# Two bands in one PSUM bank, and the projection's stores issued by SyncE

## The reference, cut to what matters

```python
# x: (16, 192, 56, 56); n = 49 tokens per window, 64 windows per image
qkv = fq(xw) @ fq(Wqkv, axis=0).T + bqkv          # xw: (1024, 49, 192), qkv: 576 columns
q, k, v = jnp.split(qkv, 3, axis=2)
q = fq(q * SCALE); k = fq(k); v = fq(v)           # three maxima over all of q, k, v
attn = fq(fq(attn) + bias); out = softmax(attn) @ v
out = fq(out) @ fq(Wout, axis=0).T + bout         # the projection, back to (16, 192, 56, 56)
# second part: depthwise 7x7 convolution, layer norm, two products with GELU and GRN,
# and the residual that was kept:  return residual + y
```

## Time and profile before

| | us |
|---|---|
| median of 3 runs | 5082.19 |
| lowest, highest | 5073.92, 5095.0 |
| the profiled execution, its own time | 5095.38 |
| its span, first to last instruction | 5093.7 |
| range stage | about 165 to 450 |
| projection stage | about 2479 to 3005 |

### The profile page before, as it was taken

The page is one execution under the profiler, slowest core; times in us unless marked ns, Lnnn a source line. Parts: engine busy times, 40 slices in busy tenths (PEclk is TensorE's granted clock), DMA queues, the critical chain, the costliest instruction groups (busy, mean ns, idle before and its releaser), DMA issues. The chain is left out here.

```text
span 5093.7 us, 116728 instructions
## 1 busy us (share of the span) xinstructions
PE 4027.8 (79%) x40394; PEld 2551.1 (50%) x40394; DVE 3922.3 (77%) x7112; ACT 3246.1 (64%) x5602; POOL 1504.5 (30%) x1844
## 2 busy tenths in 40 slices
PE   1687777676688988888456669996689999999999
PEld 1233554454577776777444434443345455554544
DVE  7797999999999999999645520001799999999985
ACT  0675777775698988989355644443556666666663
POOL 0201111111666666666422200001232222222210
PEclk9997777876799999999777779998799999999999
DMA  7773666665333333333277778886122222222212
GB/s 316 203 204 107 160 160 166 159 163 143 79 96 94 91 94 91 94 91 94 74 256 254 279 243 290 278 278 200 63 66 90 87 90 76 76 90 87 90 55 68
DMA packets 227952, 725.18 MB, mean 142 GB/s; under 512 B 30346, under 2 KB 128138, under 8 KB 206794
## 3 DMA queue, kind: packets, MB, share of 16 engines
q1 hardware_dynamic: 203402, 589.58, 39.6%
q0 software_dynamic: 24128, 130.26, 7.1%
HBM read 428.25 MB, written 291.50 MB: 141 GB/s over the span
## 5 line engine op out<-in xcount | busy, mean ns | idle before, releaser
L852 POOL TENSOR_TENSOR exp_lo<-exp,exp_hi 128x294 f16<-128x294 f32 x1024 | 773.1, 782 | 374.8 <-ACT exp_hi L923 374.8
L1613 PE MATMUL out_psum<-gelu_hi,w_parts 128*128 128x448 f16 x2016 | 605.0, 355 | 58.9 <-DVE w_parts L1789 31.5
L1649 ACT ACTIVATE gelu_pair<-h_psum,b_rows,w_unscale 128x448 f32<-128x448 f32 x448 | 324.5, 728 | 412.5 <-PE h_psum L1565 224.7
L1685 DVE BATCH_NORM_STATS2 ln_stats<-z_img 128x6 f32<-128x192 f32 x448 | 126.0, 344 | 566.7 <-DMA z_img<-zd 565.9
L1349 PE MATMUL conv_psum<-c_in,toeplitz 128*128 128x448 f16 (+1 forms) x2304 | 470.4, 366 | 68.9 <-DMA dwb<-in_L_conv_dw_b_dram 68.9
L948 DVE SCALAR_TENSOR_TENSOR logit_int<-attn_int,scalars,bias_products 128x588 f16<-128x588 int8 x512 | 488.2, 954 | 38.6 <-ACT attn_int L929 27.0
L1565 PE MATMUL h_psum<-ln_parts_T,w_hi 128*128 128x448 f16 x2016 | 494.3, 354 | 18.1 <-DVE w_in L1748 16.2
L929 ACT ACTIVATE attn_int<-p_psum,scalars 128x588 int8<-128x588 f32 x512 | 389.4, 761 | 174.7 <-PE p_psum L455 163.7
L1613 PE MATMUL out_psum<-gelu_lo,w_parts 128*128 128x448 f16 x1344 | 475.5, 354 | 0.0
L610 PE MATMUL range_psum<-q_diag,k_diag 128*128 128x196 bf16 x1536 | 275.2, 316 | 227.8 <-DVE p_min L692 225.0
L894 PE MATMUL o_psum<-a_v,exp_hi 128*128 128x34 f16 x6144 | 382.8, 179 | 78.4 <-DVE a_o L975 66.3
(11 more groups left out here) (313 smaller groups left out, 9901.8 us busy)
## 6 DMA issues: line engine op xcount, KB each, us to landing
k_diag<-kd SPq DMA_DIRECT2D x128, 384.0 KB, 5.0
toeplitz<-gd SPq DMA_DIRECT2D x48, 1024.0 KB, 17.2
yd<-y_out POOLq DMA_DIRECT2D x16, 2880.0 KB, 28.1
c_in<-yd SPq DMA_DIRECT2D x24, 1920.0 KB, 9.4
zd<-c_out POOLq DMA_DIRECT2D x24, 1792.0 KB, 13.8
z_img<-zd SPq DMA_DIRECT2D x16, 2688.0 KB, 9.4
x_chunk<-in_x_dram SPq DMA_DIRECT2D x12, 3136.0 KB, 10.4
x_img<-in_x_dram SPq DMA_DIRECT2D x16, 2352.0 KB, 15.9
```

The costliest lines, as they stand in the source:

```text
L852: last = nc.gpsimd.tensor_tensor(el[r][:, :, 2 * a, 0:N], src[:, :, a], eh[r][:, :, 2 * a, 0:N], ALU.subtract)
L1613: last = nc.tensor.matmul(po[:, t, 0:TCH], w, hx[:, f, cols], start=f == 0 and x == 0, stop=f == NF - 1 and x == len(steps) - 1)
L1649: nc.scalar.activation(h[y // 2 % 3][:, y % 2], ph[:, y % 3, 0:TCH], ACT.Gelu, scale=k1[:], bias=b1[:, f:f + 1]).then_inc(hd, 1)
```

## The change

**Range stage.** Two bands share the bank of the half-empty chunk: PAIR = 9 steps per two bands instead of 10. The ninth step writes the 64 live columns of chunk 4 for band b into partitions 0 to 63 and those of band b + 1 into partitions 64 to 127, with four matmuls of 64 weight columns. STEPS falls from 40 to 36, NG from 10 to 9. Since 9 is odd, the bank halves alternate from image to image. Five groups per image keep 8 matmuls, four have 10. The last reduction becomes two, a copy fills the scales' upper half, and the all-reduce waits for 14 links instead of 12.

**Projection stage.** (1) GpSimd quantizes units 0 and 1 before its memsets and the all-reduce, and units 2 and 3 after the all-reduce, before it issues the weights' transfers. (2) VectorE places bands 0 to 3 of image 0 before it waits for the all-reduce, and bands 4 to 7 after the chain. (3) The stores of `y_out` and `r_out` are issued by SyncE, between its loads, in a fixed order, and six units are loaded ahead of the loop. (4) The residual is stored in two parts (chunks 0 to 3, and 4 to 6), with a semaphore each; ScalarE waits for the first at x = 0 and for the second at x = 8.

```diff
@@ phase_qkv_range
-    STEPS = NWIN * NCH
+    PAIR = 2 * (NCH - 1) + 1
+    STEPS = NWIN // 2 * PAIR
...
-            pool.wait_ge(ch1, 12)
+            pool.wait_ge(ch1, 14)
...
-                        b, j, gg = n // NCH, n % NCH, n // GRP
+                        x, gg, slot = n % PAIR, n // GRP, (STEPS * k + n) % 8
...
-                        for t in range(2):
-                            rows = CK + NPART if t == 0 else CK
-                            last = nc.tensor.matmul(ps[:, n % 8, 0:BAND], s.wT[t][:, j * P:(j + 1) * P],
-                                                    xi[k][0:rows, t, b * BAND:(b + 1) * BAND], start=t == 0, stop=t == 1)
+                        b, j = n // PAIR * 2 + x % 2, x // 2
+                        whole = j < NCH - 1
+                        for lo, hi, bb in ((0, P, b),) if whole else ((0, 64, b), (64, P, b + 1)):
+                            for t in range(2):
+                                rows = CK + NPART if t == 0 else CK
+                                last = nc.tensor.matmul(ps[lo:hi, slot, 0:BAND], s.wT[t][:, j * P:j * P + hi - lo],
+                                                        xi[k][0:rows, t, bb * BAND:(bb + 1) * BAND], start=t == 0, stop=t == 1,
+                                                        skip_group_check=not whole)
...
-                        v.tensor_reduce(stat[:, gg * GRP:(gg + 1) * GRP], ps[:, gg % 2 * GRP:(gg % 2 + 1) * GRP, 0:BAND], AX.X, ALU.max,
+                        half = (NG * k + gg) % 2
+                        v.tensor_reduce(stat[:, gg * GRP:(gg + 1) * GRP], ps[:, half * GRP:(half + 1) * GRP, 0:BAND], AX.X, ALU.max,
...
@@ phase_project, SyncE
+            def store_r(m, k, part, lo, hi):
+                dst = s.rd[bass.ds(m, 1)].rearrange("i (t p) n -> (i p) t n", t=2)
+                sp.dma_start(dst[:, :, lo:hi], r[k][:, :, lo:hi]).then_inc(strr[k][part], 16)
+
+            def image(i, loads):
+                for k in range(2):
+                    m = 2 * i + k
+                    if loads(k):
+                        load(2 * m + 6, 0, False)
+                    sp.wait_ge(re, 2 * NTC * m + 2 * RTOP)
+                    store_r(m, k, 0, 0, RTOP * TCH)
+                    if loads(k):
+                        load(2 * m + 7, 1, False)
+                    sp.wait_ge(ye, NY * (m + 1))
+                    sp.dma_start(s.yd[:, :, bass.ds(m, 1)].rearrange("b p i c x q -> p (b i) (c x q)"),
+                                 y[k][:].rearrange("p (b c) x q -> p b (c x q)", c=CB)).then_inc(sty[k], 16)
+                    sp.wait_ge(re, 2 * NTC * (m + 1))
+                    store_r(m, k, 1, RTOP * TCH, TOK)
+
+            for u in range(6):
+                load(u, u % 2, u < 2)
...
@@ phase_project, ScalarE
-                        if not first and x == 0:
-                            act.wait_ge(strr[k], 16 * i)
+                        if not first and x in (0, 2 * RTOP):
+                            act.wait_ge(strr[k][x // (2 * RTOP)], 16 * i)
...
@@ phase_project, VectorE
+            dve.wait_ge(ones, 5)
+            for b in range(NWIN // 2):
+                place(0, 0, b, True)
             dve.wait_ge(ar, 1)
...
-            for b in range(NWIN):
+            for b in range(NWIN // 2, NWIN):
                 place(0, 0, b, True)
```

More of the change, by code:

```diff
@@ L405, in _ @@
             link(v.memset(sel[:, 2, 3:4], 1.0))
-            link(v.memset(sel[0:64, 2, 4:5], 1.0))
+            link(v.memset(sel[:, 2, 4:5], 1.0))
             def image(i, first):
@@ L1040, in phase_project @@
         sty = [s.sem(f"y_stored{k}") for k in range(2)]
-        strr = [s.sem(f"r_stored{k}") for k in range(2)]
+        strr = [[s.sem(f"r_stored{k}_{p}") for p in ("top", "rest")] for k in range(2)]
         oqd, tr, otd = s.sem("o_quantized"), s.sem("o_transposed"), s.sem("oT_placed")
@@ L1068, in _, with load @@
             sp.wait_ge(ones, 3)
-            def image(i, first):
-                for k in range(2):
[L1072 to L1078, removed]
+            def load(u, hf, first):
+                if not first:
+                    sp.wait_ge(oqd, u - 1)
+                for h in range(2):
+                    sp.dma_start(oi[hf][64 * h:64 * h + N], s.od[bass.ds(u, 1)].rearrange("u h n j w f -> (u h) n j w f")[h]).then_inc(ld[hf], 16)
+            def store_r(m, k, part, lo, hi):
+                dst = s.rd[bass.ds(m, 1)].rearrange("i (t p) n -> (i p) t n", t=2)
+                sp.dma_start(dst[:, :, lo:hi], r[k][:, :, lo:hi]).then_inc(strr[k][part], 16)
+            def image(i, loads):
+                for k in range(2):
+                    m = 2 * i + k
[12 more added lines that the diff above has]
+                load(u, u % 2, u < 2)
+            with sp.Fori(0, IMG // 2 - 2) as i:
+                image(i, lambda k: True)
+            image(IMG // 2 - 2, lambda k: k == 0)
+            image(IMG // 2 - 1, lambda k: False)
+            for k in range(2):
+                sp.wait_ge(sty[k], 16 * IMG // 2)
+                for part in range(2):
+                    sp.wait_ge(strr[k][part], 16 * IMG // 2)
         @blk.gpsimd
@@ L1085, in _ @@
                 link(nc.gpsimd.memset(oi[k][:], 0.0))
[L1086 to L1091, removed]
-            for x in range(2):
-                for t in range(2):
-                    nc.gpsimd.dma_start(s.gd[x, t * CK:(t + 1) * CK, :], lines[x][:, t, :]).then_inc(lst, 16)
             def quantize(u, hf, first):
@@ L1211, in _, with place @@
                 v.memset(y[k][:, :, :, QP], 0.0).then_inc(otz, 1)
+            def place(m, k, b, early):
+                dve.wait_ge(tr, NWIN * m + b + 1)
+                if not early and b == 0:
+                    dve.wait_ge(ym, NY * (m - 1))
+                    dve.wait_ge(rm, 2 * NTC * (m - 1))
+                for t in range(2):
+                    src = pt[0:CK, b % 2, :, 64 * t:64 * t + N].rearrange("p w (y x) -> p w y x", x=WS)
+                    dst = backwards(ot[k][t], 7 * b + 1, [[WS, NWIN], [PITCH, WS], [1, WS]], CK)
+                    v.tensor_scalar(dst, src, OFF, None, ALU.subtract).then_inc(otd, 1)
             dve.wait_ge(otz, 6)
```

41 lines of the change are left out of this document (20 added, 21 removed).

## The result

| | before | after |
|---|---|---|
| median, us | 5084.95 (5 runs, 5073.92 to 5095.0) | 5054.46 (5 runs, 5049.21 to 5066.06) |
| profiled span, us | 5093.7 | 5064.4 |

After / before is 0.994, 95% interval 0.9926 to 0.9953: 30.5 us faster, with 24 to 38 in the interval. The forecast was 5059, from 5082.19.

What follows compares the result with a forecast made beforehand. Reduction and round trip together bound the range stage, seven gapless DMA engines the projection stage. Terms -7.7 + 0.4 - 10 - 5 + 4.3 - 5 = -23.0 took the median 5082.19 to 5059 us, range 5037 to 5081.

Steps and rivals of the forecast that it cites:

- the term of three slots: Range stage: four narrow matmuls take three slots instead of the two of two wide ones, +0.17 us per ten-matmul group.
- The switches: Range stage: changing between full and half width loses some 0.09 us each way, +0.18 us per ten-matmul group.
- the two edge groups: Range stage: in two of four ten-matmul groups one switch falls into the wait, so each costs +0.26 us, not 0.35.
- Rival B: Range and projection stages: switches cost nothing and one queue feeds seven engines evenly, 0.5 to 1 us less per image; 5037, chance 0.20.
- The gap of 5.5: Projection start: ScalarE's 5.50 us idle for the third quantization goes, as units 2 and 3 follow the all-reduce; -5 us.
- it comes at 2510.6: Projection start: the all-reduce comes at 2510.6, 3.6 us later than now, behind two quantizations and 5.5 us of memsets.
- sign of being wrong: Projection stage: the forecast is wrong if the time per image moves by over 1 us either way.
- seven engines set the cadence: Projection loop: seven DMA engines have no gap and set the time per image, 30.4 us by the rows, 29.2 measured.
- The rise of 4.3 us in rows: Projection stores: y_out's 3072 rows take 8.70 us in the hardware queue, +0.27 per image, +4.3 us in all.
- 8.7 + 3/7 x 6.9: Projection end: y_out's rows plus the residual's remaining three sevenths, within 17.3 us from last store to next stage; -5 us.
- C (stores bring nothing): Projection stores bring nothing, or range-stage narrow matmuls do not pair: 5070 or 5081, taken at 5072 us; chance 0.18.
- D (SyncE held): Projection loop: y_out's store holds SyncE 13.7 us, loads come late, 3.75 us more per image, 5119 us; chance 0.14.

Runs made afterwards that it cites:

- e12: Changed kernel with band b + 1's two narrow matmuls left out of each shared bank, band b's kept narrow; nine reductions take 16.07 us against 16.11.
- e5: Changed kernel with two wide matmuls instead of four narrow ones per shared bank, band b + 1's last 64 columns left out; range stage 287.2 us against 298.5.
- e3: Kernel before with units 0 to 3 quantized early and bands 0 to 3 placed early, stores left with GpSimd, residual whole; ratio to before 0.9984.
- e4: Kernel before with y_out and residual stores issued by SyncE, residual in two parts, nothing early; ratio to before 0.9986.
- e2: Kernel before with the new projection stage alone; ratio to before 0.9967.
- e6: Changed kernel with each load of 49 partitions cut into 48 and 1; median 4983.2 us, ratio to before 0.9786.
- e8: Changed kernel with the residual's second part issued ahead of the y_out store; last store to stage end 12.6 us instead of 20.8.
- e10: Changed kernel with loads of 48 and 1 partitions and all stores issued by GpSimd after the image's last piece; ratio to before 0.9898.
- e7: Changed kernel with GpSimd's oT memsets ahead of the two early quantizations; first y_out piece 51.8 us after the stage's start, 4 later than in after.

## Why the prediction was right or wrong

**Sign, size and range: right.** 5054.5 lies 4.5 us under the forecast and within its own range. That it is so near is partly luck. The changed stages gained 39.4 us in the profiled pair (16 + 24 in the mean of the kernels) against 23 forecast, while the runs of the whole kernel say 24 to 38; what becomes of the rest is not shown. And the terms are off both ways: range stage, rows and missing terms brought 23 us more than forecast, start and end 7 less.

**Range stage, -7.7 forecast (-7.3 with its end), -17.0 measured: the term of three slots.** It took only the second matmul of the lower half and the first of the upper to pair. The trace of after shows both pairs, so two slots, and in e12 leaving out the upper half of them saves next to nothing. That is 0.17 us in four groups of sixteen images, 10.9 us. The switches were sized nearly right, 0.18 forecast against 0.22, and so were the two edge groups: e5 has all at 11 us, forecast 2 x 0.18 + 2 x 0.09 = 0.54 us per image, 8.6 us. Rival B came near this stage's size for another reason (free switches, three slots): switches are not free, 0.09 us each.

**Start, -15 forecast, -11.9 measured.** The gap of 5.5 went as forecast (first piece to first store, 30.0 to 24.1). The first piece came 6.0 earlier, not 10: the step "it comes at 2510.6", 31 us after the stage's start, failed. The all-reduce came after 38.3, with 7.25 us ahead of it that the profile explains by nothing. Before, such time would have lain under the wait of 10.22 us for VectorE's chain; the memsets now end after that chain and leave it open. Of the 7.2 us 4 showed, as the forecast had VectorE placing bands 0 to 3 until 34.6, behind the all-reduce; it placed them ahead of it.

**Missing term, -6.3.** From first to third store the stage gained this much more. The forecast said that the DMA engines start earlier and priced only the compute engines. e3 and e4 show that either part alone does it (57.8 to 52.1 and 50.7). Another 2.9 us came between the 13th store and the last (70.3 to 67.3); their cause is open.

**Cadence, +0.27 us forecast, -0.01 measured**, which is less than the scatter between executions. By the forecast's own sign of being wrong, 1 us either way, e2 with 31.36 would have refuted it and after not, though the code is the same. The claim that matters, that seven engines set the cadence, e6 bears out. The rise of 4.3 us in rows is not seen. The software queue's packets were 4800 bytes, not 960 (547 packets for 2.63 MB in the earlier trace rows, 220 ns each in the mean); the hardware queue's are 960 bytes of 45 ns. Per 960 bytes that is 44 against 45, and alone both ran at 350 GB/s.

**End, -5 forecast, -1.3 measured.** The step "8.7 + 3/7 x 6.9" put the residual's second part right behind `y_out`. In fact it held SyncE for 10.8 us, and the end came 10 us behind that. In e2, with the same code, it held 6.3 us and the end was 16.4, near the 17.3 forecast; e8, without it, has 12.6.

**Rivals.** B's cadence, 0.5 to 1 us less, is within what e5 and e12 read (28.6) and not after, so it is not decided. C (stores bring nothing): e4 alone is 7 us faster by its runs, with an interval that reaches no change, and up to the third store 11 us; beside the early quantization the stores add nothing up to there. e10 can't tell whether the issuing engine matters by itself, since it also changes when the stores are issued. D (SyncE held): the mechanism is there, about 21 us per image instead of the 13.7 supposed, but the cadence shows no cost. That the rows which hold SyncE are work that the seven engines have anyway would explain it; this is argued, not shown.

## What to carry to other kernels

Before moving work between queues, count the DMA engines that a transfer really uses: a share of 43% while only loads are in flight pointed to more (78 us) than the whole change gained (30 us). A stage bound by transfers gains by closing gaps in them, and two edits that do so need not add up (20.5, 11.1 and together 18.3 us up to the third store). A small transfer behind a store with thousands of rows holds the engine that issues it; at a stage's end the other order took 12.6 us instead of 20.8, in the kernel with all loads on sixteen engines it brought nothing. And where equal code scatters by 27 us in one stage, one profile doesn't price a part of a change.

## What the runs showed of the hardware

- Matmuls of 64 weight columns and 392 moving ones on the two halves start 7 ns apart, even where program order has lower, lower, upper, upper; two on the same half start 0.19 us apart (e12). A change between 128 and 64 columns costs 0.09 us each way.
- GpSimd spends 6.8 to 10.5 us without a visible instruction between a memset or tensor operation and an all-reduce (e3, after, e7), 7.0 to 7.5 behind it, and 8.6 from a memset to a tensor operation (e7).
- A transfer issued by SyncE behind 3072 rows of 960 bytes held it for 6 to 13.5 us where no loads were left and for 20 to 27 beside loads of 49 partitions.
- The same `y_out` store goes in packets of 4800 bytes when GpSimd issues it (220 ns each) and of 960 bytes when SyncE does (45 ns), at 350 and 351 GB/s.
- In the first 25 us of e8's range stage matmuls of 392 columns started every 0.33 us instead of 0.17, while the granted clock read 1.00.
- The mean time of the same 12288-byte packet in the same projection code varied from 489 to 568 ns between executions (e12, e2), at medians of 461 to 465.
